# Matrices, Toeplitz tiles and x1 tiles of a convolution kernel made and loaded at other distances

## What is computed

```python
x1 = x + einsum('bct,bcd->bdt', x, weights[cond])           # row products
K  = 2 * real(sum_n Cs[h,n] * exp(dtA[h,n] * l))            # kernel of channel h
y  = causal_conv(x1 * mask, K) + x1 * mask * D[:, None]     # mask: l < length[b]
out = x1 + y * mask
```

## Time and profile before

| | us |
|---|---|
| median of 3 runs (2347.74 to 2350.81) | 2350.06 |
| profiled execution | 2358.94 |
| its span, first to last instruction | 2357.1 |

### The profile page before, as it was taken

The page is one execution under the profiler, slowest core; times in us unless marked ns, Lnnn a source line. Parts: engine busy times, 40 slices in busy tenths (PEclk is TensorE's granted clock), DMA queues, the critical chain, the costliest instruction groups (busy, mean ns, idle before and its releaser), DMA issues.

```text
span 2357.1 us, 61717 instructions
## 1 busy us (share of the span) xinstructions
PE 2174.2 (92%) x15101; PEld 1880.7 (80%) x15101; DVE 1699.5 (72%) x3359; ACT 1505.9 (64%) x4354; POOL 1175.0 (50%) x1862
## 2 busy tenths in 40 slices
PE   6777778999999999999999999899999999999999
PEld 2222226888888888888888888799999999999998
DVE  4999204777777777777777777677777777777776
ACT  4556556777777777777777777455555555555555
POOL 0994503666666666666666666333333333333331
PEclk9999999999999999999999999999999999999999
DMA  8999999999999999999999999889989999899887
GB/s 319 420 414 369 394 359 330 316 315 315 314 316 318 317 317 318 320 315 317 320 319 311 323 316 307 241 251 262 268 253 267 266 270 259 259 261 264 254 260 223
DMA packets 337444, 716.26 MB, mean 304 GB/s; under 512 B 39554, under 2 KB 170884, under 8 KB 337412
## 3 DMA queue, kind: packets, MB, share of 16 engines
q1 hardware_dynamic: 300548, 581.66, 79.7%
q10 hardware_dynamic: 36864, 134.23, 14.0%
HBM read 395.92 MB, written 319.82 MB: 304 GB/s over the span
## 4 chain that ended last, share of the span: by engine, by line
PE 36%; DMA 28%; DVE 9%; SPq 8%; issue 8%; ACT 6%; ACTq 4%; DVEq 0%; POOL 0%
DMA decay<-x_scratch 12%; DMA toep<-k_scratch 11%; PE bank L900 7%; PE bank L902 6%; PE bank L901 6%; DMA row_x<-in_x 5%; PE bank L882 4%; DVE decay L803 4%; PE bank L945 4%; PE bank L869 3%; PE bank L937 3%; SPq L339 3%; SPq L355 2%; DVE e_lo L786 2%; ACTq L521 2%
## 5 line engine op out<-in xcount | busy, mean ns | idle before, releaser
L791 DVE TENSOR_TENSOR u_lo<-bank,u_hi 128x512 fp32r<-128x512 f32 x512 | 352.2, 688 | 252.7 <-ACT u_hi L603 246.7
L797 DVE TENSOR_TENSOR s_lo<-state,s_hi 128x128 fp32r<-128x128 f32 x768 | 291.8, 380 | 236.7 <-ACT s_hi L615 235.4
L900 PE MATMUL bank<-t_hi,u_hi 128*128 128x256 f32 x1024 | 361.7, 353 | 43.1 <-DMA toep<-k_scratch 42.5
L612 ACT ACTIVATE state<-bank 128x128 f32<-128x128 f32 x768 | 213.9, 279 | 286.8 <-PE bank L902 149.5
L803 DVE COPY_PREDICATED decay<-mask,bank 128x512 f32<-128x512 uint8 x512 | 379.1, 741 | 23.8 <-PE bank L902 3.6
L945 PE MATMUL bank<-toep,u_odd 128*128 128x128 f32 x2048 | 392.8, 273 | 0.0
L546 ACT ACTIVATE row_y<-bank 128x512 f32<-128x512 f32 x512 | 301.4, 589 | 138.2 <-ACT row_y L546 38.7
L489 POOL TENSOR_TENSOR x_lo<-row_x,x_hi 128x256 fp32r<-128x256 f32 x496 | 371.5, 778 | 0.0
L869 PE MATMUL bank<-row_x,w_sel 128*128 128x512 f32 x528 | 265.5, 630 | 94.2 <-DMA row_x<-in_x 50.2
L466 POOL TENSOR_TENSOR outer<-par 128x256 f32<-128x256 f32 x512 | 321.5, 649 | 20.5
L463 POOL COPY par<-table 128x71 f32 (+1 forms) x256 | 62.4, 244 | 540.4 <-PE bank L902 540.4
(11 more groups left out here) (139 smaller groups left out, 5456.6 us busy)
## 6 DMA issues: line engine op xcount, KB each, us to landing
row_x<-in_x SPq DMA_DIRECT2D x256, 512.0 KB, 6.1
x_scratch<-row_y ACTq DMA_DIRECT2D x256, 512.0 KB, 5.6
decay<-x_scratch SPq DMA_DIRECT2D x256, 512.0 KB, 6.4
out<-decay SPq DMA_DIRECT2D x256, 512.0 KB, 4.4
b_scratch<-b_mat SPq DMA_DIRECT2D x128, 256.0 KB, 6.5
t_hi<-k_scratch SPq DMA_DIRECT2D x256, 128.0 KB, 4.7
t_lo<-k_scratch SPq DMA_DIRECT2D x256, 128.0 KB, 4.4
b_mat<-b_scratch SPq DMA_DIRECT2D x128, 256.0 KB, 5.0
```

The lines of the kernel that those rows point to most:

```text
L791: v.tensor_tensor(u_lo[j % 2][:, blocks, :], t_bank[q][:, :].rearrange("s (k b) -> s k b", b=B), u_hi[j % 2][:, blocks, :].bitcast(fp32), ...
L900: mm(to, w_hi, m_hi, start=start, stop=False, skip_group_check=True)
```

## The change

k, K and B of a channel are made three channels ahead instead of two (`make_mats(k + 3)`, and it stands after chunk 2 instead of after the transposes), `keep_k`, `halve_k`, `split_k`, `split_b`, `keep_b` and `store_kernel` with it. Toeplitz tiles of half 0 are loaded two channels ahead instead of one, x1 tiles three instead of two. The load of an edge state waits for the last readers of its buffer only, no longer for the last y of the channel before. ScalarE copies both halves of the next row before state 1 and reads that row's condition there; e_hi of k+3 comes after state 2, and both `keep_u` come after it, before state 3. VectorE splits e of k+3 after state 2 and both u after that. Channel 2 of half 0 is made and stored ahead of the loop. The diff, where `...` stands for parts left out:

```diff
@@ -347,7 +347,8 @@
                 if isinstance(k, int) and k < H + 2:
                     sp.wait_ge(edge_saved[i], 16 * (H // 2))
                 else:
-                    sp.wait_ge(y_made, k * NQ - NQ)
+                    sp.wait_ge(s_split, k * NCH - (2 * NCH + H - 1))
+                    sp.wait_ge(s_made, k * (NCH - 1) + (H + 1 - 2 * (NCH - 1)))
                 sp.dma_start(edge[i][:, :], edge_dram[bass.ds(k - H, 1), :, :].rearrange("a n b -> (a n) b")).then_inc(edge_loaded[i], 16)
...
@@ -371,9 +372,13 @@
-            load_toeplitz(0, 0, 0, 0)
+            for k in range(2):
+                load_toeplitz(0, k, k, 0)
             sp.wait_ge(par_ready, 1)
-            for k in range(2):
+            load_x1(0, 0, 0, 0)
+            store_kernel(2, 2)
+            store_b(2, 2)
+            for k in range(1, 3):
                 load_x1(0, k, k, 0)
             for n in range(ROWS_FIRST, ROWS_FIRST + 3):
                 load_row(n, n % SLOTS, 1, n - B)
@@ -383,25 +388,25 @@
+                    if with_rows and not (isinstance(g, int) and k + 3 >= B - AHEAD):
+                        load_row(k + ROWS_FIRST + 3, j3, 1, k + AHEAD + 3)
+                    if then and then[0] == 0 and not (isinstance(k, int) and k == 0):
+                        store_b(k + 2, j2)
                     if then:
-                        load_x1(then[0], then[1], j2, then[2])
-                    if after and after[0] == 0:
-                        if not (isinstance(k, int) and k == 0):
-                            store_b(k + 1, j1)
-                        load_toeplitz(0, k + 1, j1, after[2])
-                    if then and then[0] == 1:
-                        load_toeplitz(1, k + 2, j2, then[2])
+                        load_toeplitz(then[0], k + 2, j2, then[2])
+                    if then and then[0] == 1 and not (isinstance(k, int) and k < H):
+                        load_edge(k + 2, j2)
                     if third and third[0] == 1:
                         load_b(k + 3, j3)
-                    if with_rows and not (isinstance(g, int) and k + 3 >= B - AHEAD):
-                        load_row(k + ROWS_FIRST + 3, j3, 1, k + AHEAD + 3)
-                    if then and then[0] == 0:
-                        store_kernel(k + 2, j2)
+                    if third:
+                        load_x1(third[0], k + 3, j3, third[2])
                     if seg == 0:
                         sp.wait_ge(s_ready, states_before(0, k) + NCH)
                         sp.dma_start(edge_dram[bass.ds(k, 1), :, :].rearrange("a n b -> (a n) b"), edge[j % 2][:, :]).then_inc(edge_saved[j % 2], 16)
-                    if then and then[0] == 1:
+                    if then and then[0] == 1 and isinstance(k, int) and k < H:
                         load_edge(k + 2, j2)
+                    if third and third[0] == 0:
+                        store_kernel(k + 3, j3)
                     store_x2(seg, k, j)
...
@@ -525,19 +530,19 @@
                 if q == 0:
+                    act.wait_ge(row_made, n * NQ - NQ)
                     act.wait_ge(x_loaded[j], n * 4 + (16 - j * 4))
-                ins = nc.scalar.activation(x_hi[i][:, cols], row_x[j][:, cols], ACT.Copy)
-                if q == NQ - 1:
-                    ins.then_inc(row_halved, 1)
-
-                n = m + ROWS_FIRST
-                which = act.value_load(cond_sb[0:1, bass.ds(n, 1)], min_val=0, max_val=NCOND - 1)
-                act.wait_ge(row_made, n * NQ - NQ)
+                nc.scalar.activation(x_hi[i][:, cols], row_x[j][:, cols], ACT.Copy)
+
+            def condition_of(m):
+
+                return act.value_load(cond_sb[0:1, bass.ds(m + ROWS_FIRST, 1)], min_val=0, max_val=NCOND - 1)
+
+            def halve_w(m, j, which):
+
                 w = w_all[:, bass.ds(which, 1), :].rearrange("c k d -> c (k d)")
                 nc.scalar.activation(w_sel[j][:, :], w, ACT.Copy)
-                nc.scalar.activation(w_hi[j % 2][:, :], w, ACT.Copy)
+                nc.scalar.activation(w_hi[j % 2][:, :], w, ACT.Copy).then_inc(row_halved, 1)
...
@@ -619,38 +624,39 @@
+            keep_b(2, 2)
             for q in range(NQ):
                 keep_u(0, 0, q)
-            halve_w(0, 0)
             for q in range(NQ):
                 halve_x(0, 0, q)
+            halve_w(0, 0, condition_of(0))
...
+                    j1, j3 = (j + 1) % SLOTS, (j + 3) % SLOTS
+                    after, third = later(g, j, seg, 1), later(g, j, seg, 3)
+                    next_row = with_rows and not (isinstance(g, int) and k + 1 >= B - AHEAD)
+                    if next_row:
+                        for q in range(NQ):
+                            halve_x(k + 1, j1, q)
+                        which = condition_of(k + 1)
                     if seg == 1:
                         halve_edge(k, j, g)
-                    next_row = with_rows and not (isinstance(g, int) and k + 1 >= B - AHEAD)
                     keep_s(seg, k, j, 1)
                     if next_row:
-                        halve_w(k + 1, j1)
-                        halve_x(k + 1, j1, 0)
-                    if after:
-                        keep_u(k + 1, j1, 0)
+                        halve_w(k + 1, j1, which)
                     keep_s(seg, k, j, 2)
-                    if after:
-                        keep_u(k + 1, j1, 1)
+                    if third:
+                        halve_e(third[0], k + 3, j3)
+                    for q in range(NQ):
+                        if after:
+                            keep_u(k + 1, j1, q)
                     keep_s(seg, k, j, 3)
                     if with_rows:
                         take_row(k + ROWS_FIRST, j, 0, row_bank)
-                    if next_row:
-                        halve_x(k + 1, j1, 1)
-                    if then and then[0] == 0:
-                        keep_b(k + 2, j2)
-                    if third:
-                        halve_e(third[0], k + 3, (j + 3) % SLOTS)
+                    if third and third[0] == 0:
+                        keep_b(k + 3, j3)
                     if seg == 0:
                         keep_s(seg, k, j, NCH)
                     if with_rows:
@@ -806,7 +812,7 @@
-            for k in range(2):
+            for k in range(3):
                 keep_k(k, k)
                 halve_k(k, k)
                 split_k(k, k)
@@ -820,31 +826,28 @@
+                    j1, j3 = (j + 1) % SLOTS, (j + 3) % SLOTS
+                    after, third = later(g, j, seg, 1), later(g, j, seg, 3)
+                    makes = third and third[0] == 0
                     if seg == 1:
                         split_s(seg, k, j, 0)
                     split_s(seg, k, j, 1)
-                    third = later(g, j, seg, 3)
                     if third:
-                        mats(third[0], k + 3, (j + 3) % SLOTS)
-                    if after:
-                        split_u(k + 1, j1, 0)
-                    if then and then[0] == 0:
-                        keep_k(k + 2, j2)
+                        mats(third[0], k + 3, j3)
                     split_s(seg, k, j, 2)
-                    if then and then[0] == 0:
-                        halve_k(k + 2, j2)
-                    if after:
-                        split_u(k + 1, j1, 1)
-                    if then and then[0] == 0:
-                        split_k(k + 2, j2)
+                    if third:
+                        split_e(k + 3, j3)
+                    for q in range(NQ):
+                        if after:
+                            split_u(k + 1, j1, q)
                     split_s(seg, k, j, 3)
+                    if makes:
+                        keep_k(k + 3, j3)
                     take_y(seg, k, j, 0)
-                    if then and then[0] == 0:
-                        split_b(k + 2, j2)
-                    if third:
-                        split_e(k + 3, (j + 3) % SLOTS)
+                    if makes:
+                        halve_k(k + 3, j3)
+                        split_b(k + 3, j3)
+                        split_k(k + 3, j3)
                     take_y(seg, k, j, 1)
...
@@ -966,19 +969,20 @@
                         from_chunk(k, j, c)
+                        if c == 2 and third and third[0] == 0:
+                            make_mats(k + 3, j3)
                         if c - 1 >= 1 - seg:
                             from_state(seg, k, j, c - 1)
                         if c == 0 and after:
                             pe.wait_ge(x1_loaded[j1], after[2] * 16 + 16)
                             for q in range(NQ):
                                 turn(k + 1, j1, q)
-                        if c == 0 and then and then[0] == 0:
-                            make_mats(k + 2, j2)
                         if with_rows and c % 2:
                             row_in_parts(k, j, c // 2)
                     from_state(seg, k, j, NCH - 1)
             row_groups(pe, rows, None, turn_parameters, None, None, lambda: make_mats(0, 0), lambda: make_mats(1, 1))
```

(1 more changed line is left out.)

9 lines of the change are left out of this document (2 added, 7 removed).

## The result

The changed kernel takes 2438.75 us (median of 4, 2437.42 to 2439.53), the kernel before 2349.58 us (median of 4, 2347.74 to 2350.81): a ratio of 1.037, 95% interval 1.0347 to 1.0393. The forecast was 2408 us, the range 2338 to 2455. The profiled execution took 2438.13 us with a span of 2436.3, 79.2 more than the span before.

What follows compares the result with a forecast made beforehand. TensorE was taken to pace the kernel, transfers close behind. Half 1 +27, half 0 +26 and the start +5 gave 58 us on the profiled 2358.9, so 2417, or 2408 at the median; range 2338 to 2455.

Steps and rivals of the forecast that it cites:

- waits on transfers go and waits on VectorE come: TensorE's waits on Toeplitz and x1 tiles vanish; waits on e_lo (half 0) and s_lo (half 1) replace them.
- the walks: Step-by-step timings within a channel: make_mats starts at 5.6 us in half 0; from_state(3), free at 5.81, waits 0.6.
- half 1, +27 forecast: Last from_state waits 0.6 us for s_lo of state 3 every channel; period 6.77, +27 us (bounds +14 and +39).
- half 0, +26 forecast: make_mats waits 0.65 us for e_lo, slowed by GpSimd's x_lo pieces; period 9.10, +26 us (bounds -36 and +69).
- the late condition: Half 0: ScalarE's read of the row's condition should overlap the x_hi copies; if not, 0.5 us more.
- the start, +5 forecast: Before the loop, x1 and row loads wait for channel 2's make_mats and stores; +5 us (2 to 8).
- The first rival: Old waits go and no new one comes in either half; 2264 us, chance 0.09.
- the 91 us: Gain if both transfer waits go and nothing replaces them: 42 us in half 0 plus 49 in half 1.
- Its bound for the transfers: Half 0: the transfers need 0.96 x 8.89 = 8.53 us a channel, so the period without waits is 8.55.
- The second rival: Half 0: m_mat holds w_lo back, e_lo ends earlier, wait only 0.15 us; only half 1 waits; 2346 us, chance 0.16.
- The third rival: DMA engines full at 0.96, half 0 stays 8.89 us; only half 1 and the start cost; 2382 us, chance 0.07.

Runs made afterwards that it cites:

- e2: Changed kernel plus one GpSimd wait, so the next row's split starts only once e_lo of channel k+3 is made; 2398.37 us, ratio 1.0069 to the kernel before.
- e7: Changed kernel with make_mats(k+3) behind from_state(1) instead of ahead of it; 2400.52 us, ratio 1.0232 to the kernel before.
- e1: Changed kernel with ScalarE's and VectorE's old order in half 1 only; 2430.61 us, ratio 1.0195 to the kernel before.
- e10: Changed kernel with only halve_e and split_e of half 1 moved back behind state 3; 2404.34 us, ratio 1.0239 to the kernel before.
- e8: e5 with half 0's x1 loads three channels ahead again, issued right before store_x2(k); 2290.59 us, ratio 0.9758 to the kernel before.
- second pair of runs: Changed kernel and kernel before, both run again unedited on the second and third sets' chips; 2438.43 and 2345.96 us.
- e3: Changed kernel with the edits of e1 and e2 together; 2372.58 us, ratio 0.9952 to the kernel before.
- e6: Changed kernel with only e5's order on SyncE, neither compute chain mended; 2453.48 us, ratio 1.0461 to the kernel before.
- e5: e3 plus x1 loaded two channels ahead and first, half 0's Toeplitz loads behind the edge store; 2344.26 us, ratio 0.9997 to the kernel before.
- e4: Kernel before with only its x1 loads three channels ahead, at the change's queue place; 2543.47 us, ratio 1.0686 to the kernel before.
- r_after: Changed kernel run again, unedited, on another chip; 2438.43 us, ratio 1.0397 to the kernel before.
- e9: e8 with the second half of each out tile of half 0 not stored; 2293.62 us, ratio 0.9783 to the kernel before.

## Why the prediction was right, and where it was off

**Right: that waits on transfers go and waits on VectorE come.** Both transfer waits of the earlier trace rows vanished. Both new waits stand where the prediction put them, in every channel, and the walks met them within 0.1 us: 5.70 against 5.6 in half 0, 6.40 against 6.41 (5.81 + 0.6) in half 1. e2 shows the cause in half 0 (e_lo beside a piece of x_lo), e7 that the new place of make_mats is the other half of it, e1 and e10 the cause in half 1 (e_hi ahead of the u copies, and the u copies ahead of state 3).

**Off: half 1, +27 forecast, +49 measured.** The term 128 x (6.17 + 0.6 - 6.56) priced the wait and nothing behind it. The walk's steps were steps without waits. Behind the wait TensorE needs 0.11 us more to get going, in every channel, and 0.37 us more at each turn of the loop, of which 0.27 lie ahead of the next drive and 0.10 in its first matmul. In e8, where no wait stands before the turn, it costs one 0.26 instead of 0.18 behind the first drive matmul, 0.08 in all. The average is then 6.17 + 0.59 + 0.11 + 0.37 / 4 = 6.96, measured 6.95. That TensorE's sequencer works through the turn while matmuls still run, and can't once it waits in the last matmuls ahead of it, is argued from these rows and wasn't tried by itself.

**Off: half 0, +26 forecast, +31 measured; that these are near each other is partly luck.** The prediction had 8.44 + 0.65 = 9.09 us a channel. Over channels 8 to 119 it is 8.34 (three of four channels in e8, where no wait is left in them) + 0.72 + 0.50 / 4 = 9.18, measured 9.20. The channel without waits was 0.10 too long. The wait on e_lo was 0.07 too short: TensorE was free for make_mats at 4.89 rather than 4.93, and in one channel of four, the one shown above, the pieces of x_lo began 0.1 us later than taken. The wait for state 1 at the turn of the loop, some 15 us, isn't in the sum at all. The prediction saw that advance(1) would be just met and that the read of the condition must overlap the copies ("if not, 0.5 more"), but took both for every channel from rows without the turn and left the late condition to the upper bound.

**Off: the start, +5 forecast, +3.2 measured** and 5.8 in the second pair of runs, inside its bounds of 2 to 8.

**The range.** Its bottom, 2338, isn't the sum that it names: 2350 - 36 + 14 + 5 is 2333. Nothing hangs on it here.

**The first rival (no wait comes, 2264) was wrong twice.** The waits came. And the 91 us that it took for what the change removes weren't to be had by removing them: e3 shows 8.83 and 6.82 with both chains mended. The prediction let load_x1(k+3) stand behind the landing of store_x2(k-1), and load_toeplitz(k+2) behind that of store_kernel, at no cost, though it named both. In the change this was hidden by the new waits (e6). With a compute wait mended it is the next limit: the store of out in half 1 of e1, the kernel's store in half 0 of e2 and e7, both in e3. For half 1 e5 shows it (6.82 to 6.46 with the new order on SyncE). For half 0 it is in part argued: e5 takes the waits on the kernel's store away too and stands at 8.79, with x1 tiles late, and only e8, with both mended, reaches 8.43. And e4, with the x1 load right ahead of the kernel's store, was 6.9% slower. Its bound for the transfers, 0.96 x 8.89 = 8.53 us, was wrong too: e8 runs at 8.43.

**The second rival (VectorE wins its place in half 0)** lost, but narrowly: w_lo came ahead of m_mat by 0.03 us in half of the channels, by 0.06 and 0.14 in the others, about the 0.05 us that the prediction gave the point. It is no matter of chance from channel to channel, since r_after has the same leads and the same 87 waits; but no walk with steps of 0.1 us could tell the sides apart, and that the forecast took the right one is luck.

**The third rival (transfers full at 0.96)** is refuted by e8 (0.98 and 335 GB/s, 8.43 us). e9 adds that e8 isn't bound by its bytes either (fewer, no gain).

## What to carry to other kernels

Where a change moves instructions to prefetch deeper, walk the chain of the moved ones on every engine, and look what another engine does at that moment: here two copies that were hurried ahead of a state cost more than the loads gained. On an in-order queue the place of a load counts as much as its distance: as deep as its ring it waits for the store just issued, and right ahead of a small store that others wait for it makes that one late. Put right before the next store of its ring it did neither (x1 three ahead: e4 6.9% slower, e8, with the chains mended too, 2.4% faster). A busy share of 0.96 on the DMA engines isn't a ceiling here, and the price of a short wait in every iteration includes the restart and what the wait uncovers at the turn of the loop. Where a path is just met, look at the channel at the turn by itself: its steps are not those of the others.

## What the runs showed of the hardware that was not expected

A wait of TensorE costs more than its length: 0.11 us to the next group of matmuls in half 1, and 0.37 us in all at a turn of the loop, against 0.08 where TensorE comes to it without waiting. ScalarE's sequencer took from 0.27 to 1.78 us to read one number from SBUF (e3, 600:1400), and in half 0 the turn of the loop delays ScalarE too: there x_hi starts 0.32 us later in each kernel that has the new order. The 16 DMA engines moved 335 GB/s at a busy share of 0.98 in half 0 of e8, 320 at 0.96 in e5, 307 at 0.97 in the changed kernel and 301 at 0.93 in e9: the share hardly follows the volume. The time of the kernel before depends on the chip, 2345 to 2385 us; the changed kernel gave 2438.75 and 2438.43 on two, but not on the one where the kernel before took 2385.
